# Group 1's first layer in split form: its four remainders made by VectorE during group 0

## What is computed

```python
def _cin_forward(inputs, filters):        # inputs: (512, 32 fields, 32), filters: two
    x0 = inputs
    prev = inputs
    outs = []
    for W in filters:
        z = jnp.einsum('bhd,bmd->bhmd', x0, prev)
        b, h, m, d = z.shape
        z = z.reshape(b, h * m, d)
        cur = jnp.einsum('bpd,pn->bnd', z, W[0])
        cur = jax.nn.relu(cur)
        prev = cur
        outs.append(cur)
    result = jnp.concatenate(outs, axis=1)
    return jnp.sum(result, axis=-1)
...
e = jnp.stack([tbl_0[ids[:, 0]], ..., tbl_31[ids[:, 31]]], axis=1)
z = _L0_rec_ref(e, L0_rec_filter_0, L0_rec_filter_1)
h = jnp.concatenate([z, dense_ctx], axis=1)
h = jnp.maximum(h @ W_top1 + b_top1, 0.0)
h = jnp.maximum(h @ W_top2 + b_top2, 0.0)
y = h @ W_top3
```

## Time and profile before

| | us |
|---|---|
| median of 3 runs | 834.16 (834.12 to 834.23) |
| the profiled execution | 833.78 |
| its span on the core | 832.0 |
| PE busy | 825.9 (99%) |
| ACT busy | 795.8 (96%) |
| DVE busy | 789.3 (95%) |
| POOL busy | 731.0 (88%) |

### The profile page before, as it was taken

One profiled execution on the slowest core, in us unless ns is written; L12 is line 12 of the kernel. 1 busy time (PEld: TensorE's weight loads), 2 busy tenths in 40 slices (PEclk: granted clock), 3 DMA queues, 4 the chain that ended last, 5 costly groups with the idle time before them and its releaser, 6 DMA issues.

```text
span 832.0 us, 15690 instructions
## 1 busy us (share of the span) xinstructions
PE 825.9 (99%) x3627; PEld 677.7 (81%) x3627; DVE 789.3 (95%) x2061; ACT 795.8 (96%) x2808; POOL 731.0 (88%) x550
## 2 busy tenths in 40 slices
PE   8999999999999999999999999999999999999999
PEld 6688888888888888888888888888888888888887
DVE  7799999999999999999999999999999999999996
ACT  4799999999999999999999999999999999999995
POOL 5898999989999999999999999999999999999860
PEclk9999999999999999999999999999999999999999
DMA  5541222221233221132331132221122222122000
GB/s 149 180 143 32 66 81 85 86 85 36 63 82 84 84 86 47 51 85 82 84 87 49 48 87 80 84 86 55 43 87 80 86 85 68 33 83 78 1 13 2
DMA packets 62024, 60.91 MB, mean 73 GB/s; under 512 B 26059, under 2 KB 36939, under 8 KB 61934
## 3 DMA queue, kind: packets, MB, share of 16 engines
q1 hardware_dynamic: 57838, 57.80, 23.4%
q0 software_dynamic: 4096, 2.11, 1.6%
HBM read 55.51 MB, written 4.31 MB: 72 GB/s over the span
## 4 chain that ended last, share of the span: by engine, by line
PE 97%; DMA 1%; POOL 1%; issue 0%; SPq 0%; DVE 0%; ACT 0%
PE ps_y L915 28%; PE ps_y L923 28%; PE ps_y L916 28%; PE ps_c L898 3%; PE ps_c L897 3%; PE ps_c L896 3%; POOL gat L452 1%; PE ps_c L894 1%; DMA w_raw<-w 1%; PE ps_c L885 0%; DMA gat<-table,rows 0%; PE ps_y L1019 0%; DMA ids_and_bounds_sb<-ids_and_bounds 0%; POOL w_lo L459 0%; PE ps_y L1021 0%
## 5 line engine op out<-in xcount | busy, mean ns | idle before, releaser
L571 ACT ACTIVATE prod<-ps_y,es 128x128 f32<-128x128 f32 x2560 | 754.1, 647 | 15.8 <-PE ps_y L923 15.6
L740 DVE SCALAR_TENSOR_TENSOR prod<-ps_y,es,prod 128x128 f32<-128x128 f32 x1536 | 422.6, 340 | 28.7 <-PE ps_y L923 26.4
L915 PE MATMUL ps_y<-w_hi,c_both 128*128 128x512 f32 x1024 | 402.8, 393 | 1.0 <-POOL w_lo L459 1.0
L923 PE MATMUL ps_y<-w_hi,c_both 128*128 128x512 f32 x1024 | 398.8, 390 | 0.0
L916 PE MATMUL ps_y<-w_lo,c_both 128*128 128x512 f32 x1024 | 398.6, 389 | 0.0
L441 POOL TENSOR_TENSOR prod<-prod 128x768 f32<-128x768 f32 x128 | 247.1, 1931 | 45.9 <-DVE prod L740 34.2
L752 DVE TENSOR_REDUCE csum<-prod 128x64 f32<-128x896 f32 x256 | 276.5, 1081 | 0.1
L916 PEld LDWEIGHTS ps_y<-w_lo,c_both 128*128 128x128 f32 x1024 | 192.4, 188 | 43.2 <-issue 1.0
L915 PEld LDWEIGHTS ps_y<-w_hi,c_both 128*128 128x128 f32 x1024 | 192.5, 188 | 42.9 <-issue 2.8
L923 PEld LDWEIGHTS ps_y<-w_hi,c_both 128*128 128x128 f32 x1024 | 192.2, 188 | 41.4
L431 POOL TENSOR_TENSOR z<-first,second 128x512 f32<-128x512 f32 x155 | 199.7, 1299 | 0.1
(11 more groups left out here) (122 smaller groups left out, 295.7 us busy)
## 6 DMA issues: line engine op xcount, KB each, us to landing
second<-et_scratch SPq DMA_DIRECT2D x155, 256.0 KB, 4.8
first<-et_scratch SPq DMA_DIRECT2D x31, 256.0 KB, 3.2
et_scratch<-gat SPq DMA_DIRECT2D x62, 64.0 KB
w_raw<-w SPq DMA_DIRECT2D x4, 512.0 KB, 4.7
h_scratch<-h_sums SPq DMA_DIRECT2D x120, 2.0 KB
gat<-table,rows_now POOLq DMA_INDIRECT x116, 2.4
wt_sb<-wt SPq DMA_DIRECT2D x2, 512.0 KB
rows_now<-rows SPq DMA_DIRECT2D x29, 2.0 KB, 1.7
```

The costliest lines, as they stand in the source:

```text
L571: last = nc.scalar.activation(prod[:, buffer_of(g, u), place // 2, :, place % 2], ps_y[:, bank_of(g, u, k), j * N:(j + 1) * N], ACT.Copy, ...
L740: last = nc.vector.scalar_tensor_tensor(out=summed, in0=ps_y[:, bank_of(g, u, k), j * N:(j + 1) * N], scalar=es[:, g.r, u, h:h + 1], in1=s ...
L915: nc.tensor.matmul(out, hi, w_hi, start=True, stop=False)
L923: nc.tensor.matmul(out, lo, w_hi, start=False, stop=True).then_inc(y_ready, 1)
```

## The change

`UNSPLIT` becomes 1, so group 1's four chunks run in split form too, 12 fp32r matmuls where four float32 ones stood. ACT gets four more roundings during group 0, at (1, 2), (1, 4), (1, 6) and (2, 1), and group 1's fifth moves from (2, 1) to (2, 2). DVE gets four more remainders, `rest_second`, behind whatever scaling it has at (1, 4), (1, 6), (1, 7) and (2, 4), the first three of these ahead of a half of a reduction or directly behind one another. They signal `z_lo0_ready` and a new semaphore `second_z_lo`. PE's places are unchanged. POOL's products for group 2 wait for group 1's remainders instead of for all of its layer 0.

```diff
-UNSPLIT = 2
+UNSPLIT = 1
...
-            Z_HI_AT_FIRST = {(1, 4): (2, 1)}
+            Z_HI_AT_FIRST = {(1, 0): (1, 2), (1, 1): (1, 4), (1, 2): (1, 6), (1, 3): (2, 1), (1, 4): (2, 2)}
...
             def multiply(g, k):
...
                 else:
                     pool.wait_ge(z_lo_ready, g.times(LOWS, k - LOWS))
+                    if g.times(1) == 2 and k < LASTK:
+                        pool.wait_ge(second_z_lo, k)
...
+            def rest_second(k):
+
+                dve.wait_ge(z_hi_ready, SPLIT + k + 1)
+                dve.wait_ge(l0_done, 1)
+                nc.vector.tensor_tensor(z_lo[:, k, :], z[:, k, :], z_hi[:, k, :].bitcast(F32),
+                                        ALU.subtract).then_inc(second_z_lo if k else z_lo0_ready, 1)
...
+                        if number == 0 and (u, k) in REST_SECOND_AT:
+                            rest_second(REST_SECOND_AT.index((u, k)))
...
+            REST_SECOND_AT = ((1, 4), (1, 6), (1, 7), (2, 4))
...
                 if k == 0:
                     pe.wait_ge(z_lo0_ready, g.times(1, 1 - UNSPLIT))
+                elif g.times(1) == 1 and k < LASTK:
+                    pe.wait_ge(second_z_lo, k)
```

More of the change, by code:

```diff
@@ L227, in tower @@
         z_lo0_ready = sem("z_lo0_ready")
+        second_z_lo = sem("second_z_lo")
         l0_done = sem("l0_done")
@@ L419, in split_z @@
                 nc.gpsimd.tensor_tensor(z_lo[:, k, :], z[:, k, :], z_hi[:, k, :].bitcast(F32),
-                                        ALU.subtract).then_inc(z_lo_ready, LOWS if unsplit(g) else 1)
+                                        ALU.subtract).then_inc(z_lo_ready, LOWS if g.times(1) == 1 else 1)
             def multiply(g, k):
```

## The result

| | before | after |
|---|---|---|
| median of 7 runs, us | 834.17 (833.85 to 834.36) | 842.31 (837.94 to 843.57) |
| the profiled execution | 833.78 | 837.94 |
| its span | 832.0 | 836.1 |

The ratio is 1.0094 with a 95% interval of 1.0083 to 1.0106. The change makes the kernel slower by 0.9%, 8.1 us, where I had forecast 1.1 us. No remainder of a later group was held up in this one (the longest took 0.83 us).

What follows compares the result with a forecast made beforehand. PE was taken as the bound. A late first remainder (+1.74 us), a restart (+0.12) and the split form's gain (-0.74) sum to +1.12 us, so 834.16 becomes 835.3 us, range 834.8 to 835.9.

Steps and rivals of the forecast that it cites:

- What bounds the kernel: PE, busy 99% of the span, is the bound; time taken out or idle time put in reaches the end one for one.
- The gain, -0.74 us: Group 1's four chunks cost PE 0.70 us each split instead of 0.88 unsplit, together -0.74 us (0.64 to 0.76).
- The first remainder late, +1.74: DVE's queue delays remainder 0, so PE starts group 1's chunk 0 at 32.90 instead of 31.16: +1.74 us (1.69 to 1.79).
- the restart, +0.12: PE's first two steps after idling at group 1's chunk 0 run slower than pace: +0.12 us (0.08 to 0.12).
- small second wait: A possible short PE wait at group 1's chunk 3, with a restart, allowed up to 0.35 us.
- The other three remainders, 0: Remainders 1 and 2 of group 1 come about 2 us early and remainder 3 just in time: 0 us.
- The upper end of 0.35 us: The most allowed for group 1's later remainders, a short PE wait and a restart, where 0 was taken.
- POOL and SP, cost 0: POOL's fifth remainder, fold and products come about 2 us later, but their readers are covered; SP's transfers have time: 0 us.
- A fall of the clock: Rival: idling before group 1's chunk 0 drops PE to the lower clock level, giving 837.0 us; 3%.
- The second stall: Rival: DVE or the fold of tile 2 is late, PE waits again, at chunk 3 if DVE; 836.4 us; 9%.

Runs made afterwards that it cites:

- stall_alone: The kernel before, unsplit in group 1, with four unused DVE subtractions at the four new places, for which PE waits; 835.80 us, ratio 1.0024.
- second profile: The changed kernel run once more without edits to profile it again; 842.89 us, ratio 1.0105, its profiled execution 851.03 us.

## Why the prediction was wrong

- **What bounds the kernel.** Right. PE is the bound, and every wait put into it came out at the end: 1.86 us for the 1.7 us wait of stall_alone.
- **The gain, -0.74 us.** The rows of after agree: chunk 1 of group 1 and the bank behind it last from 37.73 to 39.11, 1.38 us. By run times it is 0.4 to 0.5 us, within what they can tell.
- **The first remainder late, +1.74, and the restart, +0.12.** Right in kind and near in size: 1.35 us of wait in the first profile, 1.66 us of wait in the second profile of the changed kernel and in stall_alone, 1.86 us in the latter's time. This part and the gain together make the forecast, and with POOL's pause put in, the changed kernel comes out at 835.75, where the forecast and its small second wait reach to.
- **The other three remainders, 0.** Nearly. Remainder 1 took 1.77 to 2.33 us beside POOL, not 0.68, which made the remainders behind it late; PE waited a second time, 0.3 us in one profile and 0.85 us in the other. The upper end of 0.35 us had no room for the latter. The missing piece is the same as in the next point.
- **POOL and SP, cost 0: this step failed.** I had POOL's lateness right in kind and near in size (2.2 us forecast; the fifth remainder began at 39.08 in the second profile, 2.55 us later than before) and asked only who *reads* what POOL makes late. All of that was covered, as I said. What I did not ask was what else POOL's pauses were good for. Before, `rest_z0` found a pause of 0.24 us. What counts is by how much POOL is later than DVE, and the stall makes DVE late too. In the table above half a microsecond is enough, and my own figures had more: POOL 2.2 us late, all else 1.1. The price is a wait of 4.6 to 5.9 us and a stretch at the lower clock behind it that costs 1.8 to 2.9 us, and this is the distance from 835.3 to 842. The rows to see it in were there: the earlier trace rows has the remainder at 51.40, and in POOL's timeline the fold at 51.62 stands with 2.17 us where others take 1.85.
- **The rivals.** A fall of the clock was among them, at 3% and with the wrong cause: the 1.7 us wait did not bring it about, as the earlier trace rows had said; a wait of 4.6 us did. With the rule of the Trainium skill that I had weighed (TensorE: Matmul & The Clock Gate, "The HAM clock gate") the trace agrees for the long waits, with 0.50 behind them. The second stall was there, but at most 0.85 us. No rival held the loss.

What stays open: in group 0 a remainder that met POOL at work got in at the end of the instruction it met, although POOL did not pause (1.77 us in the second profile), and so did the one at 672.71 in the kernel before. In group 1 it had to wait for the whole queue (6.55 and 7.67). What decides between the two was not found. Of the 105 executions of the kernel before that were run beside the others, five took 840.8 to 841.8 us. Of the 82 executions of the eight kernels in which POOL waits for the remainder, none took over 837.5. That the five are the same hold-up fits, but none of them was profiled.

## What to carry to other kernels

Before an edit makes an engine late, ask not only who reads its results but also who runs in its pauses: here a VectorE instruction with two SBUF inputs ran in one of GpSimd's. Where such an instruction is on the path to the bound, a wait on GpSimd can give it its pause instead of leaving it to timing; here one wait took 6.6 us off the changed kernel and cost the kernel before nothing. And a wait of the bound engine has two prices, its own length and, when it is long, the slow stretch behind it.

## What the runs showed that I had not expected

A VectorE subtraction of 128x512 that takes 0.68 us took 7.67 us while GpSimd worked through six instructions without a pause, and a reduction of the same size at the same place took 0.67. TensorE's waits of 1.35 and 1.66 us left the granted clock at 1.00, waits of 4.55 to 5.9 us were followed by 3.8 to 6.1 us with matmuls about 0.43 us apart, the pace of the 1.2 GHz level (0.50). At the start of group 0, where PE waits for the last part of filter 1, the clock can fall too: in the first profile of the changed kernel a wait of 1.50 us and one of 0.31 us behind it, after earlier idle time, were followed by a stretch at 0.50 from 26.3 to 29.4 us, which costs about 1.7 us; before, the same two waits were 0.67 and 0.32 us and the clock stayed at 1.00:

```profile
27.00:29.00 2.00, 2.00 (x7) 1.52 (x6) 1.07 (x4) 0.55 (x3) 2.00 (x3) 0.50 0.48 155
```
